# Router logits taken out of their own block and run behind the attention's last set

## What is computed

```
x = layernorm(x + self_attention(x))            # 16 heads, causal, ALiBi
x = layernorm(x + cross_attention(x, ctx_1024)) # 16 heads
probs = softmax(x @ Wr + br)                    # router: 8 experts
gates, ids = top_k(probs, 2)
# each expert takes at most cap = 1229 tokens, by gate; others are dropped
h = silu(xg @ W1 + b1);  out = h @ W2 + b2;  y[token] += gate * out
x = layernorm(x + y)
```

## Time and profile before

| | us |
|---|---|
| runs: median of 3 (lowest to highest) | 1586.39 (1585.27 to 1587.44) |
| the profiled execution, its own time | 1587.09 |
| its span, first to last instruction | 1585.4 |
| attention block | 0 to 924 |
| logits block | 924 to 965.5 |
| route block | 965.5 to 1071 |
| experts block | 1071 to 1585 |

### The profile page before, as it was taken

The page is one execution under the profiler, slowest core; times in us unless marked ns, Lnnn a source line. Parts: engine busy times, 40 slices in busy tenths (PEclk is TensorE's granted clock), DMA queues, the critical chain, the costliest instruction groups (busy, mean ns, idle before and its releaser), DMA issues. The chain is left out here.

```text
span 1585.4 us, 43757 instructions
## 1 busy us (share of the span) xinstructions
PE 1424.7 (90%) x17886; PEld 1198.1 (76%) x17886; DVE 1019.1 (64%) x2266; ACT 990.9 (63%) x1456; POOL 619.9 (39%) x688
## 2 busy tenths in 40 slices
PE   7999999999999999999999773158999999999990
PEld 5777777777777777777777652048999999999980
DVE  5666666666677777777777647884454454454582
ACT  4677777777777677777767554205565565565563
POOL 2644444454452322222232100013455455455485
PEclk9999999999999999999999976558999999999995
DMA  6021222122221222222221174003443443443464
GB/s 195 22 62 62 62 62 61 44 61 62 62 62 57 82 66 82 82 82 82 74 79 43 58 212 102 0 11 101 97 105 48 99 102 49 100 103 50 97 240 180
DMA packets 115142, 130.72 MB, mean 82 GB/s; under 512 B 26650, under 2 KB 97084, under 8 KB 114944
## 3 DMA queue, kind: packets, MB, share of 16 engines
q1 hardware_dynamic: 100288, 106.18, 21.5%
q0 software_dynamic: 14656, 21.74, 7.9%
HBM read 83.73 MB, written 44.16 MB: 81 GB/s over the span
## 5 line engine op out<-in xcount | busy, mean ns | idle before, releaser
L527 ACT ACTIVATE at_pr<-at_A 128x2048 f32<-128x2048 f32 x128 | 240.8, 1881 | 145.5 <-PE at_A L347 145.5
L622 DVE TENSOR_REDUCE at_mx<-at_A 128x12 f32<-128x1536 f32 x128 | 224.7, 1755 | 57.6 <-PE at_A L312 54.0
L767 POOL TENSOR_SCALAR_AFFINE_SELECT at_pr<-at_pr 128x2048 f32<-128x2048 f32 x64 | 128.6, 2010 | 204.9 <-ACT at_pr L527 204.8
L1839 POOL DMA_INDIRECT total<-ex_o,ids x70 | 115.8, 1654 | 187.5 <-DVE ex_o L1767 172.5
L1708 DVE TENSOR_TENSOR ex_hT<-ex_h,ex_hT 128x384 fp32r<-128x384 f32 (+1 forms) x192 | 113.0, 589 | 98.9 <-ACT ex_hT L1641 84.9
L658 DVE TENSOR_TENSOR at_oT<-at_C,at_oT 128x512 fp32r<-128x512 f32 x64 | 44.3, 692 | 164.9 <-ACT at_oT L540 164.9
L347 PE MATMUL at_A<-at_qp,at_kt 32*128 32x256 f32 x2048 | 139.8, 388 | 0.0
L362 PE MATMUL at_C<-at_pr,at_v 128*32 128x128 f32 x4096 | 138.3, 276 | 1.0 <-ACT at_oq L534 1.0
L1640 ACT ACTIVATE ex_h<-ex_U,ex_b 128x384 f32<-128x384 f32 (+1 forms) x192 | 116.3, 606 | 33.3 <-PE ex_U L35 27.4
L362 PEld LDWEIGHTS at_C<-at_pr,at_v 128*32 128x32 f32 x4096 | 104.0, 109 | 43.3 <-issue 42.1
L35 PE MATMUL ex_U<-ex_xT,ex_w_even 128*128 128x384 f32 (+1 forms) x576 | 115.3, 360 | 5.1 <-ACT ex_hT L1641 3.5
(11 more groups left out here) (245 smaller groups left out, 3067.9 us busy)
## 6 DMA issues: line engine op xcount, KB each, us to landing
ex_w_in<-in_w SPq DMA_DIRECT2D x16, 1024.0 KB
at_turned<-in_x_turned SPq DMA_DIRECT2D x16, 512.0 KB, 4.6
at_x<-in_x SPq DMA_DIRECT2D x16, 512.0 KB, 4.0
x<-at_y SPq DMA_DIRECT2D x32, 256.0 KB, 2.3
at_x<-x SPq DMA_DIRECT2D x16, 512.0 KB, 3.9
at_turned<-in_ctx_turned SPq DMA_DIRECT2D x16, 512.0 KB, 4.6
rows<-at_y SPq DMA_DIRECT2D x32, 256.0 KB, 2.2
total<-at_y SPq DMA_DIRECT2D x32, 256.0 KB, 3.1
```

Source lines behind the costliest of these rows:

```text
L527: nc.scalar.activation(pr[:, k % 2].rearrange("p i n a q -> p (i n a q)"), A[:].rearrange("p i n a q -> p (i n a q)"), ACT.Exp).then_inc(e ...
L622: nc.vector.tensor_reduce(mx[:, k % 2, 0:12], A[:, 0:3].rearrange("p i n a k -> p (i n a) k"), AX, ALU.max).then_inc(max_done, 1)
L767: nc.gpsimd.affine_select(out=t, in_=t, compare_op=ALU.is_ge, fill=0.0, base=0, pattern=[[0, 16], [1, P]], channel_multiplier=-1).then_inc ...
L1839: nc.gpsimd.indirect_dma_start(sum_dram, bass.IndirectOffsetOnAxis(ap=ids[0:n, e, at:at + 1], axis=0), o[0:n, pr, b, :], None, bounds_chec ...
```

## The change

The logits have no block of their own. `logits_programs` makes, inside the attention's block, the same steps as functions, and each engine calls them behind its own tail:

- Memory: T uses the four banks of the attention's A; the two banks of L are B[1] and C[0]; those of B are C[1] and B[0]; xT is the attention's sT. The buffers wr_s, zero and lT stay their own.
- PE goes on to T(0), T(1) behind `output(63)`. Ahead of L(0) it waits for the split matrix and for the last residual.
- ACT copies T(0) and T(1), and only then runs `normalise(63)`; the bias of group 0 comes behind it.
- DVE splits the matrix between `rest_o(63)` and `residual(63)`, and starts with the logits behind `deviation(63)`.
- SP clears the spare rows and issues the loads of groups 4 and 5 ahead of `store(63)`, the other ten loads behind it. A load also waits for the y stores of its rows.

The diff, cut (steps that only changed their names or places are left out):

```diff
@@ attention_layers @@
+        load_rows, clear_rest, rest_cleared, tensor_program, scalar_program, split_matrix, vector_program = logits_programs(
+            nc, c, layer_groups, [A[:, i].rearrange("p n a k -> p (n a k)") for i in range(4)], [B[1], C[0]], [C[1], B[0]], sT,
+            logits_inputs, logits, iota8, consts["iota8"], rows_dram, x2_outs[1])
...
+            def load_later(i):
+                for u in (2 * (layer_groups + i), 2 * (layer_groups + i) + 1):
+                    sp.wait_ge(y_stored[u % 4], stored_before(u + 4))
+                load_rows(sp, i)
+
             store(halves_of - 2)
+            clear_rest(sp)
+            load_later(LOGIT_LOADS)
+            load_later(LOGIT_LOADS + 1)
             store(halves_of - 1)
+            for i in range(LOGIT_LOADS + 2, layer_groups):
+                load_later(i)
             for u in range(halves_of - 4, halves_of):
                 sp.wait_ge(y_stored[u % 4], stored_before(u + 4))
+            rest_cleared(sp)
...
             output(halves_of - 1)
+            tensor_program(pe, lambda engine: engine.wait_ge(res_done, halves_of))
...
-            normalise(halves_of - 1)
+            scalar_program(act, lambda: normalise(halves_of - 1))
...
             rest_o(halves_of - 1)
+            split_matrix(dve)
             residual(halves_of - 1)
             deviation(halves_of - 1)
+            vector_program(dve)
@@ logits_programs, in place of logits_block @@
+    def load_rows(sp, g):
+        sp.wait_ge(turned, g - LOADS + 1)
+        sp.dma_start(x2[:, g % LOADS], rows_dram[g * G:(g + 1) * G, 0:D]
...
+    def clear_rest(sp):
+        sp.wait_ge(wr_ready, 1)
...
+    def tensor_program(pe, last_sum):
+        pe.wait_ge(const_in, 48)
...
+        for g in range(groups):
+            pe.wait_ge(x_loaded[g % LOADS], 16 * (g // LOADS + 1))
+            if g >= 2:
+                pe.wait_ge(d_copied, 2 * (g - 1))
...
+            last.then_inc(turned, 1)
+            if g == 1:
+                pe.wait_ge(wr_ready, 1)
+                last_sum(pe)
+            if g >= 1:
+                logits_of(g - 1)
+            if g >= 2:
+                back(g - 2)
...
+    def scalar_program(act, last_normalise):
...
+            for half in range(HALVES):
+                nc.scalar.copy(xT[:, g % 2, 0, half, :], T[2 * (g % 2) + half]).then_inc(a_copied, 1)
+            if g == 1:
+                last_normalise()
+            if g >= 1:
+                add_bias(g - 1)
@@ decoder_layer @@
-            logits_block(nc, tokens // P, rows, total, inputs, logits, iota8, ins["iota8"])
```

More of the change, by code:

```diff
@@ L850, in inputs_of_logits, with logits_programs @@
     return inputs
-def logits_block(nc, tiles, rows_dram, sum_dram, inputs, logits, iota8, iota8_dram):
-    groups = tiles // NB
+def logits_programs(nc, c, groups, T, L, B, xT, inputs, logits, iota8, iota8_dram, rows_dram, sum_dram):
     LOADS = LOGIT_LOADS
[L858 to L912, removed]
@@ new lines, in logits_programs @@
+    wr_s = c.enter_context(nc.sbuf_tensor("lg_wr_s", [P, HALVES, 2, E], FP32R))
+    zero = c.enter_context(nc.sbuf_tensor("lg_zero", [P, D + E], FP32))
+    lT = c.enter_context(nc.sbuf_tensor("lg_lT", [2 * E, 2, G], FP32))
+    ident, wr, br, x2, const_in, x_loaded = (inputs[name] for name in ("ident", "wr", "br", "x2", "const_in", "x_loaded"))
+    lb = [b[0:2 * E, :] for b in L]
+    bb = [b[:, 0:NB * 2 * E].rearrange("p (n a e) -> p n a e", n=NB, a=2) for b in B]
+    wr_hi = c.enter_context(nc.semaphore("lg_wr_hi"))
@@ new lines, in tensor_program, with add_bias @@
+            if g == 1:
[3 more added lines that the diff above has]
+                logits_of(g - 1)
+            if g >= 2:
+                back(g - 2)
+        logits_of(groups - 1)
+        back(groups - 2)
+        back(groups - 1)
+    def scalar_program(act, last_normalise):
+        def add_bias(g):
+            act.wait_ge(l_full, g + 1)
+            if g >= 2:
+                act.wait_ge(b_full, g - 1)
+            nc.scalar.activation(lT[:, g % 2, :], lb[g % 2], ACT.Identity, bias=br[:, 0:1]).then_inc(l_done, 1)
+        act.wait_ge(const_in, 48)
+        for g in range(groups):
+            act.wait_ge(turned, g + 1)
+            if g >= 2:
+                act.wait_ge(l_full, g - 1)
+            for half in range(HALVES):
+                nc.scalar.copy(xT[:, g % 2, 0, half, :], T[2 * (g % 2) + half]).then_inc(a_copied, 1)
[3 more added lines that the diff above has]
+                add_bias(g - 1)
+        add_bias(groups - 1)
@@ new lines, in split_matrix, with vector_program, take @@
+    def split_matrix(dve):
+        nc.vector.memset(zero[:], 0.0)
+        dve.wait_ge(const_in, 48)
+        nc.vector.tensor_copy(wr_s[:, :, 0, :], wr[:]).then_inc(wr_hi, 1)
+        dve.wait_ge(wr_hi, 1)
+        nc.vector.tensor_tensor(wr_s[:, :, 1, :], wr[:], wr_s[:, :, 0, :].bitcast(FP32), ALU.subtract).then_inc(wr_ready, 1)
+    def vector_program(dve):
+        def take(g):
+            dve.wait_ge(b_full, g + 1)
+            nc.vector.tensor_reduce(logits[:, g * NB:(g + 1) * NB, :], bb[g % 2].rearrange("p n a e -> p n e a"),
+                                    AX, ALU.add).then_inc(b_done, 1)
+        for g in range(groups):
+            for half in range(HALVES):
+                dve.wait_ge(a_copied, 2 * g + half + 1)
+                nc.vector.tensor_tensor(xT[:, g % 2, 1, half, :], T[2 * (g % 2) + half],
+                                        xT[:, g % 2, 0, half, :].bitcast(FP32), ALU.subtract).then_inc(d_copied, 1)
+            if g >= 2:
+                take(g - 2)
+        take(groups - 2)
+        take(groups - 1)
@@ L1924, in decoder_layer @@
                              {k: ins["attn_" + k] for k in ("wq", "wk", "wv", "wo")},
-                             {k: ins["xattn_" + k] for k in ("wq", "wk", "wv", "wo", "bq", "bk", "bv", "bo")}, ins, inputs)
-            logits_block(nc, tokens // P, rows, total, inputs, logits, iota8, ins["iota8"])
+                             {k: ins["xattn_" + k] for k in ("wq", "wk", "wv", "wo", "bq", "bk", "bv", "bo")}, ins, inputs, logits, iota8, rows)
         moe(nc, tokens, cap, ins, rows, total, out, logits, iota8)
```

42 lines of the change are left out of this document (38 added, 4 removed).

## The result

| | us |
|---|---|
| changed kernel, median of 4 (lowest to highest) | 1576.93 (1576.35 to 1578.37) |
| kernel before beside it, median of 4 | 1586.91 (1585.27 to 1587.77) |
| ratio, 95% interval | 0.9941 (0.9926 to 0.9956) |
| its profiled execution, its span | 1576.95, 1575.2 |

The medians differ by 10.0 us, the ratio gives 9.4 (7.0 to 11.7). Later, on another chip than that of experiments 1 to 8, the same pair gave 1573.92 (5 runs) and 1581.79 (11 runs), ratio 0.9945 (0.9932 to 0.9958), 7.9 us by the medians and 8.7 by the ratio. The measured values of the gain lie between 8 and 10 us; the forecast was 8.9. One execution of experiment 7's kernel, marked slow, took 2782.75 us where its five others took 1570 to 1573; the ratios leave it out, and no record tells its cause.

A forecast was written before the change was run, and what follows sets the result against it. PE bounds the full logits pipeline, behind an idle hole from 916.1 to 924.7 us. Border 8.6 plus clock 0.3, other terms 0, gives 8.9 us: 1586.39 to 1577.5 us, range 1575.6 to 1581.0.

The forecast's parts named there:

- Step 1: Start of the logits: without the block border T(0) starts at 916.15, 8.6 us earlier, with 0.05 us for the hand-over.
- Step 2: From T(0) to L(0) at the same clock: the fill keeps its 4.09 us, so L(0) starts at 920.24.
- Step 3: TensorE's clock during T(0): back at 917.4, making L(0) 0.3 us earlier, at 919.95; bounds 0 and 0.74 us.
- Step 4: ACT's queue: normalise(63) behind the copies just fits before T(2)'s copy, cost 0; with a late clock 0.6 us lost.
- Steps 5 and 7: DVE's clearing and splitting under the wo matmuls costs 0, without that cover 0.5 us; other banks and another buffer cost 0.
- Step 6: SP's queue: loads behind the last store still arrive in time, group 6 with 0.5 to 3.0 us spare; cost 0.
- A: Start of the logits: the clock comes back late, L(0), T(2), L(1) run slow; gain 5.7 us, 1580.7; chance 0.12.
- B: SP's stores and loads 4 to 6 crowd, T(6) waits 2 to 4 us; 1579.4 to 1581.4 us; chance 0.06.
- C: Start of the logits: T(0) or L(0) still waits for the tail, the whole hole stays; 1586.4 us; chance 0.03.
- D: Throughout the logits the clock never comes back, each group costs 1.5 us more; 1600 us, slower; chance 0.02.

The follow-up runs named there:

- experiments 1 to 8: Eight follow-up variants, three of the kernel before and five of the changed kernel, varying waits, engine orders, transposes or filler; 1573.49 to 1591.58 us on that chip.
- experiment 7: Changed kernel with 7 and 5 matmuls of zeros in PE's two tail pauses; 1576.70 us, ratio 0.9931; later 1572.29 us, ratio 0.9933.
- Experiments 1 to 3: Kernel before with the split moved early, 1586.68 us; without the wait for the last stores, 1583.78; changed kernel with the last normalisation before the logits, 1583.66.
- second profile: Changed kernel itself, unaltered, run and profiled once more on another chip; 1573.92 us, ratio to the kernel before 0.9945.
- experiment 5: Changed kernel, but ACT runs the last normalisation ahead of its copies of T(0) and T(1), as before; median of 9 1582.15 us, ratio 0.9969.
- experiment 6: Changed kernel, but SP issues the last store first, all twelve loads and three small transfers behind it; median of 4 1578.12 us, ratio 0.9936.

## Why the prediction was right

The bound and its place were read correctly: routing starts 9.49 us earlier, and all of it comes from L(0), 9.62 us earlier, less 12 x 0.011 = 0.13 of longer groups.

- *Step 1, the border.* Predicted 8.6 with a hand-over of 0.05; T(0) moved by 8.97, since the hand-over came to -0.20 against the modelled end of the matmuls, and the attention ended 0.10 earlier in this profile. Experiments 1 to 3 show that the hole was a chain: 0.49 split, 2.04 wait for the landing, 4.02 the border with both, 4.85 the tail's arithmetic with the hand-over.
- *Step 2, the fill,* kept its length: 4.05 us in the second profile with the clock late (920.43 - 916.38), against 4.09.
- *Step 3, the clock.* Forecast back at 917.4 and L(0) 6.8 us after the wo start. Measured: about 916.3 and 6.17 in one profile, about 919.5 and 6.77 in the other. I took one value for what varies from run to run: the clock came back 3.2 and 5.8 us after the wo matmuls began, where I had 4.2. The two bounds given, 0 and 0.74 us, held the first profile's 0.65. That was near the best to be had: in experiment 7, with T(0) and T(1) wholly at the high clock (1.91 us), L(0) is at E + 3.12, against E + 3.24.
- *Step 4, ACT's order.* The cost of 0 held in both profiles. In the first profile ACT even waited 0.27 us before the normalisation, for POOL's shift, where I had said that it would not. The 0.6 us that I added for a late clock didn't show. In the second profile, with the transposes at 3.41 us, the copy of T(2) came at T(0) + 6.06, where my chain had 922.8 - 916.15 = 6.65. T(1)'s copy started 0.24 sooner (T(0) + 3.45, not 3.69), and from there on ACT took 2.61 us (919.83 to 922.44), not 2.94: its rows overlap by 0.1 where I had added gaps. What the step undersold is that the order is needed: without it 3.3 us are lost, and the clock's fall on top (experiment 5).
- *Steps 5 and 7:* DVE's split ran at 913.01 to 913.53 under the wo matmuls. Other banks and the shared buffer cost 0.011 us a group, which I had put at 0.
- *Step 6, SP's order.* No PE wait on a load, but loads 4, 5 and 6 took 6.0, 6.5 and 5.7 us to land, between my two bounds of 4.9 and 7.4. Load 4 landed at 917.16 + 6.0 = 923.2, 1.5 us before T(4) at 924.71; load 6 at 921.59 + 5.7 = 927.3, 2.0 before T(6) at 929.31. It was tightest where I hadn't looked, at group 4, and experiment 6, which issues load 4 at E + 6.1 instead of E + 1.2, turns that into a wait.
- *Rivals.* A: the pause before L(0) was 1.28 us and the clock stayed up; behind a pause of 4.59 us it fell (experiment 5). B: no load was late. C: T(0) waited for nothing of the tail, and L(0) only by way of DVE's rests, which start where the variance ends (917.79). D: the clock was at 1.00 from 919.2 to 950.

The sum was 8.9 where routing moved by 9.49 us, at the upper edge of the 8.0 to 9.5 that I had given the forecast. The misses are the hand-over (0.25), the attention's earlier end (0.10), the clock (0.36) and, the other way, the longer groups (0.13). That the median came within 0.6 us of 1577.5 is luck in part. The changed kernel's profile had 0.64 us more from the experts' clock, while the kernel before ran 0.5 us slower beside it than in the runs I started from. With the late clock of the second profile routing would have gained some 0.6 less, and the forecast would have held as well.

## What to carry to other kernels

Here a border between blocks cost what the slowest engine still had to do, and the landing of the last stores, for work that needed none of it: look for the first instruction behind the border and ask what data it waits for. Taking the border away is only half; each engine's own order must then let the new work pass the old tail, here above all ACT, where one step in the old place gave back 4 to 5 of the 9 to 10 us. Once the border is gone, the tail's pauses can take the next stage's first steps: with the transposes there L(0) came 4.2 to 4.6 us sooner after the wo matmuls' start, and the time fell clear of the noise. Filling the pauses with matmuls of zeros instead went with an L(0) 1.3 to 2.0 us sooner in the traces, and no gain in time clear of the noise.

## What was not expected of the hardware

- Transposes alone, after 8.66 us of idle time, brought TensorE's clock from 1.2 to 2.4 GHz within about 3.0 us.
- The same program has the clock fall and rise at different places: in the experts' first 60 us it stood at the low level for 4 to 12 us, and in the attention's tail of the kernel with early transposes it fell in one profile (last wo matmuls 2.79 us) and not in the other (1.69). In the changed kernel itself it came back at about 916.3 in one profile and 919.5 in the other. A time from one run can't carry a theory about 1 us; distances in the trace can.
- In all nine profiles with the logits in the attention's banks and buffer a group takes 2.303 to 2.305 us, in the four with tiles of their own 2.293 to 2.295. The 0.01 us stand between the start of the products L and the start of the transposes back B, on average over 11 groups 1.105 to 1.109 us against 1.096 to 1.099; the step of the transposes T is no longer than before (0.85). The cause is open: no run separates the banks from the buffer.
